# Keeping the residual stream mean-free: centering only in the first and third layer norm

## What is computed

```
x = conv0(x); x = conv1(x)              # expert-mixed 1x1, depthwise 3x3, 1x1, batch norms, + x
t = tokens(x)
t = t + attn(ln(t))                     # norm 0: linear attention, output weights Wff, bff
t = t + ffn0(ln(t))                     # norm 1: 24 -> 96 -> 24, fp8 products, fp16 sums
t = t + fourier(ln(t))                  # norm 2: 24 -> 48, FFT over tokens, mix, inverse FFT, w2, batch norm
t = t + ffn1(ln(t))                     # norm 3: as ffn0
ln(t) = (t - mean(t)) / sqrt(var(t) + 1e-5)
```

## Time and profile before

| | |
|---|---|
| Three runs | 2530.13, 2531.35 (median), 2535.86 us |
| Profiled execution: span from first to last instruction | 2537.7 us |
| Its time beyond the span | not among the figures; the span ends with the last store, landed 6.0 us after its issue |
| PE / PEld busy | 2164.1 us (85%) / 1225.5 us (48%) |
| DVE busy | 1921.6 us (76%) |
| ACT busy | 1664.5 us (66%) |
| POOL busy | 114.0 us (4%) |
| Mean granted TensorE clock | 0.907 of full |
| DMA | 12 GB/s mean |

### The profile page before, as it was taken

How to read it: one execution, slowest core, us unless ns; L and a number is a source line. 1 busy time by engine, 2 the same in 40 slices (tenths; PEclk the granted TensorE clock), 3 DMA queues, 4 the chain that set the end, 5 groups by cost and what they waited for, 6 DMA issues and landing times.

```text
span 2537.7 us, 49162 instructions
## 1 busy us (share of the span) xinstructions
PE 2164.1 (85%) x19776; PEld 1225.5 (48%) x19776; DVE 1921.6 (76%) x3719; ACT 1664.5 (66%) x2822; POOL 114.0 (4%) x290
## 2 busy tenths in 40 slices
PE   3777988999889987999879996899889998987765
PEld 2233433664346633664336643476336643663652
DVE  4976978798968797798948896886967989456153
ACT  3344456876787677776777676765877758757645
POOL 1000000000000000000000000000000000000000
PEclk9887979999889989999989997998999999987866
DMA  5001000000020001100020002000010000000000
GB/s 140 1 1 20 1 1 11 10 2 1 1 39 2 2 1 28 13 2 1 1 39 2 2 1 39 1 2 1 1 30 3 2 1 1 21 1 1 21 1 20
DMA packets 108595, 29.57 MB, mean 12 GB/s; under 512 B 104145, under 2 KB 104273, under 8 KB 107985
## 3 DMA queue, kind: packets, MB, share of 16 engines
q1 hardware_dynamic: 108368, 26.41, 5.2%
HBM read 16.77 MB, written 9.63 MB: 10 GB/s over the span
## 4 chain that ended last, share of the span: by engine, by line
PE 42%; DVE 35%; ACT 12%; issue 6%; SPq 3%; DMA 1%; ACTq 0%; DVEq 0%
DVE acc L1440 16%; PE P L741 7%; PE P L722 6%; PE P L787 5%; PE P L938 4%; SPq L582 3%; DVE SQ L1582 3%; PE P L951 2%; PE P L979 2%; PE P L763 2%; DVE arena L1566 2%; PE P L778 2%; PE P L993 2%; PE P L889 1%; DVE arena L1582 1%
## 5 line engine op out<-in xcount | busy, mean ns | idle before, releaser
L1440 DVE SCALAR_TENSOR_TENSOR acc<-H,Dm,acc 128x784 f32<-128x784 f32 x1024 | 989.5, 1028 | 72.8 <-ACT acc L1106 72.4
L722 PE MATMUL P<-T,Wk 112*128 112x448 f32 (+1 forms) x768 | 379.9, 587 | 56.0 <-DVE biasT L1421 28.0
L741 PE MATMUL P<-H,diag 64*64 64x392 f32 x4608 | 402.8, 499 | 12.7 <-DVE T L1456 12.7
L1099 ACT ACTIVATE H<-P,biasA 128x448 f32<-128x448 f32 (+1 forms) x384 | 236.1, 621 | 188.9 <-PE P L722 106.7
L741 PEld LDWEIGHTS P<-H,diag 64*64 64x64 f32 x4608 | 172.2, 135 | 225.6 <-issue 202.6
L787 PE MATMUL P<-T,pack_b 112*112 112x448 f32 x448 | 232.0, 610 | 24.0 <-DVE T L1541 9.7
L722 PEld LDWEIGHTS P<-T,Wk 112*128 112x128 f32 x768 | 129.3, 198 | 178.1 <-ACT H L1099 86.6
L1129 ACT ACTIVATE acc<-P,biasT 128x392 f32<-128x392 f32 x128 | 68.6, 584 | 177.7 <-PE P L741 177.7
L963 PE MATMUL P<-pack_b,arena 128*96 128x112 f32 x928 | 112.1, 270 | 22.3 <-DVE roots L1582 11.7
L1106 ACT ACTIVATE acc<-H,Dm 128x784 f32<-128x784 f32 x128 | 121.9, 953 | 13.1 <-PE P L763 11.1
L938 PEld LDWEIGHTS P<-pack_b,arena 113*64 113x64 f32 x1792 | 113.5, 215 | 27.7 <-issue 19.6
(11 more groups left out here) (194 smaller groups left out, 3715.7 us busy)
## 6 DMA issues: line engine op xcount, KB each, us to landing
xin<-in_x SPq DMA_DIRECT2D x224, 42.0 KB, 2.3
out_y<-arena SPq DMA_DIRECT2D x8, 1176.0 KB, 6.0
pack_b<-in_pack_b SPq DMA_DIRECT2D x1, 3820.5 KB, 17.5
arena<-in_pack_s SPq DMA_DIRECT2D x1, 1548.0 KB, 8.6
pack_a<-in_pack_a SPq DMA_DIRECT2D x1, 1084.0 KB, 5.4
pack_i<-in_pack_i SPq DMA_DIRECT2D x1, 320.0 KB, 3.1
arena<-in_pack_k SPq DMA_DIRECT2D x1, 192.0 KB, 3.2
```

Source lines behind the costliest of these rows:

```text
L722: pe.matmul(conv_rows(slice(0, 128), HB[(NP * s + e) % len(HB)], n), Wk1[:, 128 * j:128 * (j + 1)], image_rows(T[q % 3], a, n), start=True ...
L741: last = pe.matmul(conv_rows(slice(64 * h, 64 * (h + 1)), CVB + r, HH), diag[64 * r:64 * (r + 1), tap, :], H1[64 * r:64 * (r + 1), slot(s, ...
L1099: act.activation(H1[:, slot(s, j), o:o + n, 1:1 + HW], conv_rows(slice(0, 128), HB[(NP * s + e) % len(HB)], n), ACT.Relu, bias=biasA[:, j, ...
L1440: ins = ve.scalar_tensor_tensor(a, H1[:, slot(s, j), r:r + SR, c:c + HW], Dm[:, j, tap:tap + 1], a, ALU.mult, ALU.add)
```

## The change

From norm 0 on, T holds the centred stream: norms 0 and 2 write the centred chunk back to T, and norms 1 and 3 have no centering at all, because the weights of the two branches ahead of them (attention output, Fourier projection) are made mean-free in the setup. The mean that the output needs is kept in four of the 16 padding rows (MR = 12 to 15), to which both branches add theirs, and the output's transposes become matmuls by a matrix that adds it back. In detail:

- norms 1 and 3: no L787, no L1147; the squares read T. ScalarE waits for the additions to T itself. Norm 2's wait for GpSimd's fill goes from ScalarE to VectorE.
- attention: banks 4, 3, 4, 3, 3, 3, 3 for the seven output matmuls up to the last quad, since norm 1's variance, which begins earlier now, sums in bank 4; four banks in turn in the last. One more column in one small matmul and one more small VectorE operation.
- Fourier: fw2 has 2 + 48 columns; S2 has 100 columns for a k instead of 96, evacuated by two instructions instead of one.
- output: matmul against "rest" (112x96) in place of a transpose (112x112).
- setup: 17 more small VectorE operations, each waited for; larger constant packs; a smaller dynamic_dma_scratch_size.

```diff
 def attention_banks(q):
-        return (MB[:1], MB) if q < NQ - 1 else (MB[:1] + CB, MB + CB)
+        free = MB[:1] if q < NQ - 1 else MB[:1] + CB
+        out = MB[::-1] + MB[::-1] + 3 * MB[:1] if q < NQ - 1 else (free + free)[:NCK]
+        return free, out
...
# tensor, layer_norm
                 def variance(c):
+                    if n == 1 and c == 0:
+                        pe.wait_ge(at_added.sem, at_added.at(q, 3))
                     pe.wait_ge(norm.sq_ready.sem, norm.sq_ready.at(q, N0 + c + 1))
...
-                    pe.matmul(P[0:R, cen[c % NC], 0:CK], par["cen"][0:R, :], T[q % 3][:, CK * c:CK * (c + 1)],
-                              start=True, stop=True).then_inc(norm.cen_psum.sem, 1)
+                    if i == 0:
...
+                        pe.matmul(P[0:R, cen[c % NC], 0:CK], par["cen" if n == 0 else "cenk"][0:R, :],
+                                  T[q % 3][:, CK * c:CK * (c + 1)], start=True, stop=True).then_inc(norm.cen_psum.sem, 1)
...
# tensor, attention
-                    if c >= len(ab):
-                        pe.wait_ge(at_added.sem, at_added.at(q, c - len(ab) + 1))
+                    if ab[c] in ab[:c]:
+                        pe.wait_ge(at_added.sem, at_added.at(q, c - ab[:c][::-1].index(ab[c])))
...
# tensor, output_transposes
-                        last = pe.transpose(P[0:BLK, FB[g % BN], R * s:R * (s + 1)], by_token_block(T[q % 3])[:, BPG * g + s, :],
-                                            par["ident"][0:R, 0:R])
+                        last = pe.matmul(P[0:BLK, FB[g % BN], RC * s:RC * (s + 1)], by_token_block(T[q % 3])[:, BPG * g + s, :],
+                                         par["rest"][0:R, :], start=True, stop=True)
...
# scalar, layer_norm
+                    D = T[q % 3][:, CK * c:CK * (c + 1)]
+                    if i == 0:
+                        act.wait_ge(norm.cen_psum.sem, norm.cen_psum.at(q, c + 1))
+                        act.activation(D, P[0:R, cen[c % NC], 0:CK], ACT.Copy).then_inc(norm.d_ready.sem, 1)
+                        act.wait_ge(norm.d_ready.sem, norm.d_ready.at(q, c + 1))
+                    elif n == 1:
+                        act.wait_ge(at_added.sem, at_added.at(q, c + 1))
+                    elif c == 0:
+                        act.wait_ge(fo_added.sem, fo_added.at(q, NFO))
...
# scalar, fourier
-                    act.activation(S2[:, KG * g:KG * g + n, :],
-                                   P[0:KR, FB[g % BN], 0:n * RC].rearrange("p (s n) -> p s n", s=n),
+                    s2 = P[0:KR, FB[g % BN], 0:n * PK].rearrange("p (s j n) -> p s j n", s=n, j=2)
+                    act.activation(S2[:, KG * g:KG * g + n, 0:QI].rearrange("p s (j n) -> p s j n", j=2), s2[:, :, :, 0:2], ACT.Copy)
+                    act.activation(S2[:, KG * g:KG * g + n, QI:PK].rearrange("p s (j n) -> p s j n", j=2), s2[:, :, :, 2:2 + 2 * CH],
                                    ACT.Copy).then_inc(s2_ready.sem, 1)
...
# vector, setup (centre_columns is called three times, centre_rows twice, and two products stand ahead of them)
+            def centre_columns(mean, w):
+                n = mean.shape[1]
+                w = w.rearrange("p (i c) -> p i c", i=n)
+                link(ve.tensor_reduce(mean, w, AX.X, ALU.add))
+                link(ve.tensor_scalar(mean, mean, 1.0 / CH, None, ALU.mult))
+                link(ve.tensor_tensor(w, w, mean.unsqueeze(2).broadcast_to([w.shape[0], n, CH]), ALU.subtract))
+            def centre_rows(bias, values, m):
+                link(ve.tensor_reduce(m, values, AX.X, ALU.add))
+                link(ve.tensor_scalar(m, m, par["sgn"][0:R, :], None, ALU.mult))
+                link(ve.tensor_tensor(bias, bias, m, ALU.add))
...
# vector, attention
+                ve.tensor_tensor(bdw[2][:, MR:PAD], P[0:R, MB[0], 128 + CH:128 + CH + 1].broadcast_to([R, QI]),
+                                 par["maskI"][0:R, :], ALU.mult)
```

More of the change, by code:

```diff
@@ L31 @@
 PAD = 64 - 2 * CH
+MR = PAD - QI
+PK = QI + RC
 R = PAD + RC
@@ L216, with __init__ @@
 class Norm:
-    def __init__(self, n, D, SQ, banks):
-        self.n, self.D, self.SQ, self.banks = n, D, SQ, banks
+    def __init__(self, n, SQ, banks):
+        self.n, self.SQ, self.banks = n, SQ, banks
     def small(self, room, thirds):
@@ L358, in build @@
         Yf = mid[0:R, 0:TOK]
-        normM = Norm(n=0, D=Yf, SQ=z[0:R, 0:2 * CK], banks=middle_banks)
+        normM = Norm(n=0, SQ=z[0:R, 0:2 * CK], banks=middle_banks)
         normM.small(z[:, 2 * CK:], sb("thirdsm", [96, LT, LN_N], BF16))
@@ L372, in build @@
         Y = arena[0:R + 1, reg1:reg1 + 64 * HW]
-        normB = Norm(n=2, D=Y, SQ=SQ[0:R, :], banks=back_banks)
+        normB = Norm(n=2, SQ=SQ[0:R, :], banks=back_banks)
         roots = sb("roots", [128, CK])
@@ L470, in build @@
         for half, norm, layers in (("middle", normM, 2), ("back", normB, 2)):
-            norm.cen_psum = sig(f"centred_in_psum_{half}", layers * NCK)
-            norm.d_ready = sig(f"centred_ready_{half}", layers * NCK)
+            norm.cen_psum = sig(f"centered_in_psum_{half}", NCK)
+            norm.d_ready = sig(f"centered_ready_{half}", NCK)
             norm.sq_ready = sig(f"squares_ready_{half}", layers * NCK)
@@ L765, in conv_out, with layer_norm @@
                     last.then_inc(cv_psum.sem, 1)
-            def layer_norm(q, norm, n, written):
+            def layer_norm(q, norm, n, written=None):
                 i = n - norm.n
@@ L921, in middle @@
                 yield from attention(q)
-                yield from layer_norm(q, normM, 1, at_added)
+                yield from layer_norm(q, normM, 1)
                 yield from ffn(q, 0, normM)
@@ L992, in fourier @@
                         o = 2 * HW * (k % 4)
-                        last = pe.matmul(P[0:R, FB[g % BN], o:o + 2 * HW], S2w[:, RC * k:RC * k + R], par["g"][0:KR, k, :],
+                        last = pe.matmul(P[0:R, FB[g % BN], o:o + 2 * HW], S2w[:, PK * k:PK * k + R], par["g"][0:KR, k, :],
                                          start=True, stop=True)
@@ L1038, in back @@
                 yield from fourier(q)
-                yield from layer_norm(q, normB, 3, fo_added)
+                yield from layer_norm(q, normB, 3)
                 yield from ffn(q, 1, normB)
@@ L1138, in layer_norm @@
                 i = n - norm.n
-                D, (cen, var, _) = norm.D, norm.banks(q, n)
+                cen, var, _ = norm.banks(q, n)
                 NC = len(cen)
@@ L1481, in layer_norm @@
                         stand(ve)
-                    ve.tensor_tensor(dst[0:R, CK * c:CK * (c + 1)], norm.D[0:R, CK * c:CK * (c + 1)],
+                    if n == 2 and c == 0:
+                        ve.wait_ge(fpads_set.sem, fpads_set.at(q, 1))
+                    ve.tensor_tensor(dst[0:R, CK * c:CK * (c + 1)], T[q % 3][:, CK * c:CK * (c + 1)],
                                      P[0:R, spread[c % NSP], 0:CK], ALU.mult, saturate=False).then_inc(norm.y_ready.sem, 1)
@@ L1642, in _shape_constants @@
     live = np.arange(PAD, R)
+    c["cen"][live, MR + com_i] = 1.0 / CH
+    c["cenk"] = c["cen"] + np.diag((np.arange(R) >= MR) & (np.arange(R) < PAD))
+    c["rest"] = np.concatenate([np.zeros((MR, RC)), np.arange(QI)[:, None] == com_i[None, :], np.eye(RC)])
+    c["sgn"] = np.where(np.arange(R) < MR, 0.0, np.where(np.arange(R) < PAD, 1.0, -1.0))[:, None] / CH
     selv = np.zeros((R, 32 + (NCK - 1) * QI))
@@ L1738, in _parameters @@
     p["fri"] = np.tile(np.stack([np.diagonal(m["r"]), np.diagonal(m["i"]), m["rb"], m["ib"]], axis=1), (2, 1))
-    p["fw2"] = blocks(m["w2"].T, 2)
+    p["fw2"] = np.pad(blocks(m["w2"].T, 2), ((0, 0), (2, 0)))
     p["fbn2f"] = np.tile(np.stack([np.tile(m["bn2_gamma"], 2), np.tile(m["bn2_var"], 2)])[None], (R, 1, 1))
-    p["fbn2"] = np.stack([m["bn2_" + k] for k in ("gamma", "beta", "mean", "var")], axis=1)[row_c]
+    p["fbn2m"] = np.tile(np.stack([m["bn2_beta"], m["bn2_mean"]])[None], (R, 1, 1))
+    p["fbn2"] = below(np.stack([m["bn2_" + k] for k in ("gamma", "beta", "mean", "var")], axis=1)[com_c])
     return p
```

66 lines of the change are left out of this document (35 added, 31 removed).

## The result

The changed kernel takes 2624.6 us (median of 4 runs, 2618.76 to 2628.24) against 2531.64 us before: 1.0354 times as long, interval 1.0337 to 1.0371. The forecast was 2499 us. The profiled execution took 2623.52 us, its span is 2621.4 us.

The account below looks back on a forecast made before the run. No engine was taken as the bound alone: the order of turns hands the chain between PE (42%), DVE (35%) and ACT (12%). -56 + 10 + 6 + 8 = -32 us gave 2499 us from the median; range 2455 to 2530.

Parts of the forecast that it names:

- Part 3: Output by matmul instead of transposes: +0.18 us for each of 56 groups, 10 us of PE, 6 us on the chain.
- The upper bound of +44 us: Output matmul: the cost if every second instruction costs a full transpose, 56 x 0.79 us.
- Part 2: Attention's output matmuls c = 4 to 6 wait for the addition just before: 22 us of PE, 10 us taken.
- Part 1: No centering in norms 1 and 3: 116 us less PE work, 68.5 us of it on the chain, 56 us freed.
- Part 4: Small things: setup 4.1, larger pack 0.5, attention's extra DVE operation 2, extra ACT evacuations 1.7; 8.3 us slower in all.
- the quarter held back for DVE: Outside the tail, 12.4 of 49.7 us freed were taken as lost where a shorter PE runs into a full DVE.
- the prediction's own signs of being wrong: DVE idles less but the span stays, PEclk falls in windows like 1175 us, or L863's waits exceed 40 us.
- the rival: TensorE's clock falls with less work in 13 stretches beside norms 1 and 3: 40 us slower, 2539 us; chance 0.05.
- In the tail the sum had 18.8 us: After 2236 us, three norms 1 or 3 lose their centering: 3/4 of L787's 25.1 us on the chain.
- DVE takes over: All 49.7 us outside the tail run into DVE's taps, PE's costs hidden alike: -10.5 us, 2521 us; chance 0.20.
- PE sets the time everywhere: All 116 us of removed PE work count, against some 16 us of costs: -100 us, 2431 us; chance 0.07.
- The single bank: L863 at c = 4 to 6, 21 waits at 3.5 us each: +31 us, 2562 us, slower; chance 0.08.

Follow-up runs that it names:

- both undone: Changed kernel with the output's transposes again (channel mean left out) and attention's output in two banks again: 2528.1 us, 0.9966 of before.
- the matmuls kept: Kernel with both undone, plus the 112 centering matmuls of norms 1 and 3 issued on PE with no reader: 2530.99 us, 0.9983 of before.
- shorter taps: DVE's taps cut from 14 to 12 rows, in the kernel before: 2508.8 us, 0.9911; in that with both undone: 2479.22 us, 0.9799.
- GpSimd's additions of 112x384: Whole version: both undone, ACT copying the mean columns and GpSimd adding them to the output before its store: 2544.36 us, 1.0046 of before.

## Why the prediction was wrong

**What failed first: Part 3, the size of the output matmul.** It was priced at 0.97 us for a group instead of 0.79, 10 us of PE in all and 6 us on the path. Measured are 1.60 us against 0.45 us at full clock, and 65 to 68 us on the time. Two faults are in that step. The 0.79 us for four transposes was read in the tail. The window there shows the half clock, while the two rows that it was set against are from full clock; all three are in the earlier trace rows, without their clocks. Windows of the kernel before:

```profile
461.00:463.00 2.00, 2.00 (x19) 1.32 (x18) 0.00 (x0) 1.95 (x3) 0.00 (x0) 1.00 0.00 0
579.00:581.00 2.00, 2.00 (x20) 1.20 (x14) 1.93 (x6) 0.00 (x0) 0.00 (x0) 1.00 0.00 0
2352.00:2357.00 5.00, 4.72 (x26) 4.72 (x27) 0.23 (x1) 2.45 (x5) 0.00 (x0) 0.50 0.00 0
```

So even at 0.97 us the step was 0.52 us a group at full clock and not 0.18. And the weights of the new matmul lie 28 floats apart. L1016's are adjacent, and L938's 64 strided columns, scaled by their number, give 0.121 us for 112 columns, where this load takes 0.200. The transposes take the same strided columns of T with one load of 0.104 us a block, the fp32 matmul with two of 0.200 us. Why the stride doubles the matmul's load and not the transpose's is not shown. The upper bound of +44 us, a second full transpose, was the right thought and also read at half clock and still too small. The row of the Trainium skill ("FP8 and Floating Point Precision", TensorE Precision Notes) from which the prediction's estimate of 0.64 us a group by four passes came was further off than the rows, against 1.60 us measured: the load of the weights sets the pace here, and such a count doesn't see it.

**Part 2, the single bank: the mechanism right, the size off.** 32 us measured alone and 33 us in the changed kernel, against 10 us, inside the bounds of 0 to 36. The choice of 42% of 22 us was the error: PE's 22.7 us of waits cost more than themselves, since DVE can wait in turn, as at 2126.99 us. Over 21 waits it is 1.5 to 1.6 us each.

**Part 1, the freed time: 56 us forecast, and some 12 us measured.** 8.6 us are left after the setup's 4; the other 4 us of Part 4 were not measured, and if they cost what was forecast, the norms gave 17 us. It is the step from the chain's share to a gain that failed, and the quarter held back for DVE was far too little. The instructions went as told. But PE's busy time fell by 71 us only (2164.1 to 2092.8), not by 116: the same remaining work took 45 us longer, and the mean clock was 0.894 against 0.907. The rest found three takers: DVE, PE's waits ahead of a convolution, and the clock. Only DVE's share, some 20 us, was measured; how the rest divides stays open.

Norm 1 lies beside the taps. From 1175 to 1200 us DVE was busy for 24.71 us before and PE for 24.77 us. With both undone DVE is still nearly full, and PE has room:

```profile
1175.00:1200.00 25.00, 21.88 (x157) 8.19 (x153) 23.30 (x43) 14.05 (x24) 4.13 (x6) 0.86 0.00 1
1200.00:1225.00 25.00, 23.16 (x195) 9.41 (x188) 24.64 (x45) 15.26 (x26) 1.75 (x7) 1.00 0.01 2
```

The clock in the first window is 0.86, where it was 1.00 before: one of the prediction's own signs of being wrong. It is 1.00 again in the same window with the matmuls kept. The chain there was PE's, but DVE was a hair behind it; a chain names one of two that are tied. With shorter taps the same edit gains 20 us more.

Norm 3 lies where PE waits for the next convolution's weights. Waits of PE in the kernel before (us in total, times, longest), and then with both undone:

```profile
PE P L722 <- DVE biasT L1421: 28.0, 11, 5.1
PE P L722 <- ACT H L1099: 27.2, 42, 1.6
PE P L741 <- DVE T L1456: 12.7, 7, 5.2
```

```profile
PE P L726 <- ACT H L1106: 37.8, 62, 1.6
PE P L726 <- DVE biasT L1456: 36.1, 14, 5.2
PE P L745 <- DVE T L1491: 18.0, 12, 6.2
```

24 us of what was freed are found again in these three waits around a convolution's start and in it, with the releasers unchanged: PE comes earlier and waits longer for the same operation. With the matmuls kept the same three waits are 70.9 us again, against 91.9 us without them and 67.9 us before.

And in such a gap the clock falls. Windows of the changed kernel at the start of a convolution with a line of its timeline, and then the same of the kernel before:

```profile
1486.00:1489.00 3.00, 0.33 (x8) 0.08 (x8) 2.86 (x12) 0.97 (x2) 0.00 (x0) 0.89 0.00 0
1489.00:1492.00 3.00, 2.65 (x18) 1.08 (x18) 1.56 (x5) 0.69 (x2) 1.15 (x1) 0.50 0.02 5
1492.00:1495.00 3.00, 3.00 (x23) 1.52 (x20) 0.00 (x0) 2.08 (x4) 0.00 (x0) 0.50 0.01 3
```

```profile
1489.35 1.86 PE L726 MATMUL P<-T,Wk 112*128 112x448 f32 x2 [3.03 <-DVE biasT L1456]
```

```profile
1453.50:1456.50 3.00, 2.51 (x21) 0.86 (x20) 2.84 (x13) 2.52 (x6) 0.00 (x0) 1.00 0.00 0
1459.50:1462.50 3.00, 3.00 (x23) 1.05 (x21) 0.00 (x0) 2.79 (x6) 0.00 (x0) 1.00 0.00 0
```

```profile
1454.68 1.01 PE L787 MATMUL P<-T,pack_b 112*112 112x448 f32 x2
```

Before, the centering matmuls kept PE busy while it would have waited, and it went into the convolution at full clock; afterwards it is idle for 2.7 of 3 us and goes in at half. The first tap of that convolution keeps its distance to the kernel before (32.5 us). The Trainium skill names this ("TensorE: Matmul & The Clock Gate", HAM oscillation): gaps of PE bring back the half clock. The prediction held one window against that rule and gave the rival 0.05; these windows agree with the rule (PE busy for 0.33 of 3.00 us, then clock 0.50). The price in that rival, 40 us, is too high all the same: with the matmuls kept the clock is back at 0.911, and the kernel is no faster.

In the tail the sum had 18.8 us. From the last convolution on it is 9 us (the last tap comes 4 us earlier, the end of the span 13 us). The last norm 3 gave its 5.2 us, so the other two gave under 4 us together. The lower clock of the tail's windows above fits that: with the matmuls put back the end comes only some 3 us later against the last tap.

**The rivals.** *DVE takes over* was the right reading of Part 1, at -10.5 us for the norms, the setup and the small parts together, where 8.6 us were measured. It held PE's costs to be hidden alike, and there it failed: cover for work that goes is no cover for work that comes, because the output's matmuls and the bank's waits lie where PE is on the path. *PE sets the time everywhere* has a slip in its sum: 16 us of costs leave Part 4's 8 us out, so it was 2439 us and not 2431. *The single bank* ended on the right side at 2562 us; it had 3.5 us a wait where 1.6 were measured, and Part 3 was what carried the time beyond it.

**What held.** The setup (4.1 us forecast, 4.2 measured at the first tap), the counts (L794 x224), DVE's share of the chain (35 to 41%), a wait of L870 for L1563 of about 20 us (22.7 us as PE's matmuls show it), and the last norm 3, though at 5.2 us and not under 5.

## What to carry to other kernels

A line's share of the chain is not what its removal gives: where two engines are both full, the chain names one of them, and here a window of 25 us with both at 24.7 us was the sign that the other is next. Price an instruction from a row at the same clock and with the same layout of weights, and look at both rows of PE, matmuls and weight loads: here the loads were busy throughout and set the pace. Work given to an idle engine can slow a busy one: compare the busy engine's operations where the two overlap, not their mean over the run. A small gain that is bought with costs elsewhere should have each cost measured alone first: here 0.9966 was bought with 1.0259 and 1.0126.

## What was not expected of the hardware

A weight load of 112 fp32 columns that lie 112 bytes apart, for a fp32 matmul, comes every 0.200 us at clock 1.00 and at 0.50; the same with adjacent columns every 0.099 us at 1.00 and every 0.187 us at 0.50; the transposes of the same strided columns every 0.104 us and 0.187 us. The first window of a strided output stage is at 0.71 and the next at 0.50 although PE's column is full (3.00 of 3.00), while with adjacent columns it is 1.00 at the same quad; but in another quad (1909 us) the strided form ran at 1.00. In the 2 us ahead of the first case PE was busy for 0.80 us, ahead of the stage with adjacent columns for 0.87 us, so a gap alone doesn't tell them apart. Beside GpSimd's additions of 112x384 a tap of DVE took up to 1.61 us instead of 1.03, and a tensor_scalar of 128x448 in fp16 0.90 us instead of 0.33. Of the 56 additions, those with DVE idle took 0.83 us; 12 took 1.56 to 11.62 us, all of them with DVE busy for at least 92% of the time (spans on POOL are rough).
